# Exponentials of 1024 columns over a ring of two PSUM buffers, in attention with an interleaved projection

## What is computed

```python
xn = layernorm(x)
k, q, v = split(xn @ W_kqv.T, 3)                 # 16 heads of 64
bias = slope[h] * (n - s)                        # slope[h] = 2 ** (-(h + 1) / 2)
score = einsum('bhsd,bhnd->bhsn', q, k) / 32 + bias
s = einsum('bhsn,bhnd->bhsd', softmax(score), v) # keys n, queries s
g = silu(ffn(xn))                                # 3 cycles of a coupling network
out = x + s * g
```

## Time and profile before

| | us |
|---|---|
| median of the runs (2 runs, 2830.49 and 2832.97) | 2831.73 |
| profiled execution | 2836.87 |
| its span on the slowest core (core 1) | 2835.3 |
| spans of the 8 cores | 2811.7 to 2835.3 |

### The profile page before, as it was taken

One profiled execution on the slowest core, in us unless ns is written; L12 is line 12 of the kernel. 1 busy time (PEld: TensorE's weight loads), 2 busy tenths in 40 slices (PEclk: granted clock), 3 DMA queues, 4 the chain that ended last, 5 costly groups with the idle time before them and its releaser, 6 DMA issues.

```text
span 2835.3 us, 32583 instructions; the slowest of 8 cores (2811.7 to 2835.3 us)
## 1 busy us (share of the span) xinstructions
PE 2166.7 (76%) x8756; PEld 903.1 (32%) x8756; DVE 826.9 (29%) x1315; ACT 1466.6 (52%) x2366; POOL 100.7 (4%) x150
## 2 busy tenths in 40 slices
PE   0235889899899988998888855788888888854665
PEld 0232233233233223332222214433333333323444
DVE  1556323121111001010000006345345345345333
ACT  0220555768788898889999950133333333332000
POOL 1000000000000000000000000000000000002332
PEclk9667999999999899999999985799999999985555
DMA  9600211000000000000000024444444444433665
GB/s 186 164 30 8 49 28 23 16 11 14 8 8 8 8 8 8 1 9 8 8 9 9 8 56 163 123 108 104 102 110 101 104 110 99 107 72 128 195 194 177
DMA packets 343974, 190.21 MB, mean 67 GB/s; under 512 B 303419, under 2 KB 321981, under 8 KB 343694
## 3 DMA queue, kind: packets, MB, share of 16 engines
q1 hardware_dynamic: 323470, 160.08, 21.5%
q0 software_dynamic: 3696, 11.27, 2.8%
q10 hardware_dynamic: 16640, 16.78, 2.2%
HBM read 165.30 MB, written 36.96 MB: 71 GB/s over the span
## 4 chain that ended last, share of the span: by engine, by line
PE 46%; ACT 16%; DVE 15%; issue 11%; DMA 5%; DVEq 5%; POOL 1%; ACTq 1%; SPq 0%; another core or an unknown queue 0%; POOLq 0%
ACT PBUF L467 14%; PE PA L705 13%; PE PC L459 4%; PE PA L459 4%; PE PA L374 3%; PE PC L374 3%; PE PD L441 3%; DMA XT<-x 3%; PE PBp L441 3%; PE PD L443 2%; DVE STATE L821 2%; DVE TMP L812 2%; DVE SBF L790 2%; DVEq L824 2%; DVEq L818 2%
## 5 line engine op out<-in xcount | busy, mean ns | idle before, releaser
L467 ACT ACTIVATE PBUF<-PC,ebias_s 128x512 bf16<-128x512 f32 x977 | 665.0, 777 | 183.6 <-PE PC L459 115.1
L467 ACT ACTIVATE PBUF<-PA,ebias_s 128x512 bf16<-128x512 f32 x967 | 658.6, 774 | 139.3 <-PE PC L459 88.1
L459 PE MATMUL PC<-QT,KT 64*128 64x512 bf16 x977 | 344.7, 385 | 75.3 <-ACT PBUF L467 54.7
L705 PE MATMUL PA<-SBF,W1S 128*128 128x512 bf16 x1536 | 359.5, 398 | 25.6 <-DVE SBF L790 21.9
L459 PE MATMUL PA<-QT,KT 64*128 64x512 bf16 x967 | 317.3, 387 | 41.2 <-ACT PBUF L467 20.2
L716 ACT ACTIVATE H<-PA,b1c_s 128x512 bf16<-128x512 f32 x192 | 131.9, 687 | 348.1 <-PE PA L705 348.1
L812 DVE TENSOR_TENSOR TMP<-PD,STATE 128x512 f32<-128x512 f32 x192 | 123.7, 686 | 362.9 <-PE PD L804 357.5
L441 PE MATMUL PD<-PBUF,VB 128*65 128x512 bf16 x528 | 207.7, 393 | 27.1 <-ACT PBUF L467 17.0
L705 PEld LDWEIGHTS PA<-SBF,W1S 128*128 128x128 bf16 x1536 | 154.6, 102 | 230.7 <-issue 69.2
L487 DVE COPY SRW<-PBp 65x1024 f32<-65x1024 f32 x32 | 39.1, 1221 | 605.9 <-PE PD L443 605.9
L443 PE MATMUL PD<-PBUF,VB 128*65 128x512 bf16 x528 | 207.2, 392 | 0.0
(11 more groups left out here) (109 smaller groups left out, 1837.0 us busy)
## 6 DMA issues: line engine op xcount, KB each, us to landing
W1S<-w1b_s SPq DMA_DIRECT2D x192, 256.0 KB, 2.9
W2S<-w2b_s SPq DMA_DIRECT2D x96, 256.0 KB, 2.8
XTs<-x SPq DMA_DIRECT2D x8, 2048.0 KB, 28.1
sraw_s<-SRW SPq DMA_DIRECT2D x64, 256.0 KB
XT2s<-x SPq DMA_DIRECT2D x16, 1024.0 KB, 5.2
XT<-x SPq DMA_DIRECT2D x32, 512.0 KB, 4.1
SINB<-sraw_s ACTq DMA_DIRECT2D x16, 1024.0 KB, 6.2
out<-OUT SPq DMA_DIRECT2D x32, 512.0 KB, 2.9
```

The lines of the kernel that those rows point to most:

```text
L459: inst = TE.matmul(RING[r], lhs, QT[b][hh * 64:(hh + 1) * 64, sc * SC2:(sc + 1) * SC2], start=True, stop=True)
L467: inst = SE.activation(out=PB_[slot][:], in_=RING[r], func=AF.Exp, bias=ebias[:, h * 32 + nt: h * 32 + nt + 1], scale=1.0 / 32.0)
L705: inst = TE.matmul(HALF[slot][:], W1S[wslot][:, ft * 128:(ft + 1) * 128], sbf[:, ft * TC:(ft + 1) * TC], start=(ft == 0), stop=(ft == NF - 1))
```

## The change

Two neighbouring exponentials of a head become one. The ring is handed out to the attention in whole buffers, PA or PC (`ring_next_pair`): if the position is odd, it is rounded up to the next even one, a half being passed over; TensorE then waits for the tokens of both halves. Both score matmuls of a head are issued, only the second counts up tSC, and one ScalarE instruction reads 128x1024 out of PSUM and writes a buffer PBH of 1024 columns. Six PBH lie over the same bytes as the twelve PBUF. The two products read the two halves of PBH, and the tokens of both halves of the ring name that one exponential. The projection units still take single halves by `ring_next`. The order of the matmuls on TensorE is as before.

```diff
--- before.py
+++ after.py
@@ -132,6 +132,7 @@
     QT = [at(f"QT{i}", [128, S], BF16, 128 + 8 * i) for i in range(2)]
     VB = [at(f"VB{i}", [128, 32 * 130], BF16, 144 + 8.25 * i) for i in range(2)]
     PB_ = [at(f"PBUF{i}", [128, 512], BF16, 160.5 + 1 * i) for i in range(12)]
+    PBH = [at(f"PBH{i}", [128, 1024], BF16, 160.5 + 2 * i) for i in range(6)]
     SRW = [at(f"SRW{i}", [128, 1024], F32, 172.5 + 4 * i) for i in range(2)]
     VSTG = [at(f"VSTG{i}", [128, 512], F32, 180.5 + 2 * i) for i in range(2)]
     vsj = [0]
@@ -338,6 +339,19 @@
                 TE.wait_ge(sem.h, val)
             return r
 
+        PFULL = [PA, PC]
+
+        def ring_next_pair():
+            r = ring_pos[0]
+            if r % 2:
+                r = (r + 1) % 4
+            for q in (r, r + 1):
+                if ring_tok[q] is not None:
+                    sem, val = ring_tok[q]
+                    TE.wait_ge(sem.h, val)
+            ring_pos[0] = (r + 2) % 4
+            return r
+
         OUTH = [[PBp[0:65, 0:512], PBp[0:65, 512:1024]],
                 [PD[0:65, 0:512], PD[0:65, 512:1024]]]
         out_tok = [(vXBe, max(lnslot_tok[2], lnslot_tok[3])), None]
@@ -415,8 +429,8 @@
 
         SC2 = 512
         NSCP = 4
-        pb_av_tok = [0] * 12
-        pb_exp_tok = [0] * 12
+        pb_av_tok = [0] * 6
+        pb_exp_tok = [0] * 6
         srw_tok = [0, 0]
         sridx = [0]
 
@@ -431,21 +445,20 @@
                 def emit_attnv(flush=False):
                     while pend:
                         hh, pnt, pj = pend.pop(0)
-                        s0 = hh * 6 + (pj % 3) * 2
-                        TE.wait_ge(sExp.h, pb_exp_tok[s0 + 1])
+                        s0 = hh * 3 + (pj % 3)
+                        TE.wait_ge(sExp.h, pb_exp_tok[s0])
                         if not started[hh] and out_tok[hh]:
                             osem, oval = out_tok[hh]
                             TE.wait_ge(osem.h, oval)
                         st = not started[hh]
                         stop = flush and all(x[0] != hh for x in pend)
                         TE.matmul(OUTH[hh][0], v4[b][:, pnt, hh, 0:65],
-                                  PB_[s0][:], start=st, stop=stop)
+                                  PBH[s0][:, 0:512], start=st, stop=stop)
                         inst = TE.matmul(OUTH[hh][1], v4[b][:, pnt, hh, 0:65],
-                                         PB_[s0 + 1][:], start=st, stop=stop)
+                                         PBH[s0][:, 512:1024], start=st, stop=stop)
                         started[hh] = True
                         tAV.inc(inst)
                         pb_av_tok[s0] = tAV.n
-                        pb_av_tok[s0 + 1] = tAV.n
 
                 for nt in range(N0_PAIR[p], NT):
                     for hh in range(2):
@@ -453,23 +466,25 @@
                         if nt < N0[h]:
                             continue
                         lhs = KT[b][hh * 64:(hh + 1) * 64, nt * 128:(nt + 1) * 128]
+                        rp = ring_next_pair()
                         for sub in range(2):
                             sc = 2 * scp + sub
-                            r = ring_next()
-                            inst = TE.matmul(RING[r], lhs,
+                            inst = TE.matmul(RING[rp + sub], lhs,
                                              QT[b][hh * 64:(hh + 1) * 64, sc * SC2:(sc + 1) * SC2],
                                              start=True, stop=True)
-                            tSC.inc(inst)
-                            SE.wait_ge(tSC.h, tSC.n)
-                            slot = hh * 6 + (jj[hh] % 3) * 2 + sub
-                            if pb_av_tok[slot]:
-                                SE.wait_ge(tAV.h, pb_av_tok[slot])
-                            inst = SE.activation(out=PB_[slot][:], in_=RING[r], func=AF.Exp,
-                                                 bias=ebias[:, h * 32 + nt: h * 32 + nt + 1],
-                                                 scale=1.0 / 32.0)
-                            sExp.inc(inst)
-                            pb_exp_tok[slot] = sExp.n
-                            ring_tok[r] = (sExp, sExp.n)
+                        tSC.inc(inst)
+                        SE.wait_ge(tSC.h, tSC.n)
+                        slot = hh * 3 + (jj[hh] % 3)
+                        if pb_av_tok[slot]:
+                            SE.wait_ge(tAV.h, pb_av_tok[slot])
+                        inst = SE.activation(out=PBH[slot][:], in_=PFULL[rp // 2][:],
+                                             func=AF.Exp,
+                                             bias=ebias[:, h * 32 + nt: h * 32 + nt + 1],
+                                             scale=1.0 / 32.0)
+                        sExp.inc(inst)
+                        pb_exp_tok[slot] = sExp.n
+                        ring_tok[rp] = (sExp, sExp.n)
+                        ring_tok[rp + 1] = (sExp, sExp.n)
                     emit_attnv()
                     for hh in range(2):
                         if nt >= N0[2 * p + hh]:
```

## The result

The changed kernel takes 2891.35 us (median of 11 runs) against 2833.79 of the kernel before in the same series (10 runs); the ratio is 1.0205, with a 95% interval of 1.0189 to 1.0221. It is about 58 us slower, and the interval lies on both sides of 2%. The forecast was 2845, in a range of 2800 to 2885, and gave 0.82 to "within 2%". In some runs of either kernel the cores of one die have a lower clock and the run takes some per cent longer; the ratios leave such runs out, the medians do not.

The account below looks back on a forecast made before the run. ScalarE's exponentials bound steps without projection units, TensorE sets the pace with them; after the change a two-step buffer chain would. Terms −10.8 + 8.8 + 6.4 + 4.7 + 4 = +13 us on 2831.7 give 2845, range 2800 to 2885.

Parts of the forecast that it names:

- S0a to E0: In each step, from head 0's first score matmul to its exponential: 0.22 + 0.54 us.
- the alternation of short and long steps: Steps without projection units: S0 (head 0's score matmuls) starts at 0, 2.02, 4.53, 6.55 us and so on.
- the saving of 0.30 a step: Each two-head step: two wide exponentials for four narrow save 0.30 us, of which only 0.05 comes through.
- A: Rival, faster: in two-head steps the saving arrives whole, only engine rates count; 2742 us, chance 0.08.
- C: Rival, slower: an exponential's second PSUM bank costs a second access, +0.15 us on 444 steps; 2912 us, chance 0.04.
- Costed at nothing: Items priced at zero: single-head steps, two ring waits for one naming the same count, fewer ScalarE waits and increments.
- 4.53: Chain over two steps without units, through exponentials, score matmuls and attention-value products: 4.53 us, so 2.27 a step.
- −7.4 of pair 7: Pair 7's four strips without projection units: 73.5 us each against 75.34, −1.85 each.
- the +4 that was forecast: Pairs 0 to 3: 48 two-head steps at up to 0.2 us each and 16 short strips; bounds 0 and 10.
- rival B: Slower: TensorE's clock falls in a strip's first steps, pairs 4 to 7, 1.6 us lost a step; 2947 us, chance 0.06.
- its sign: What would show the clock falling: granted clock in pairs 6 and 7, now 0.99, below 0.95.
- the gains that I had subtracted: Pair 6: −1.2 us for strip ends and steps after the last unit, −1.85 for its strip without units.

Follow-up runs that it names:

- e2_coarse_narrow: e1_one_wait with two exponentials of 512 columns in place of each one of 1024, the ring still coarse; ratio 1.0399 to the kernel before.
- e5_wait_order: e1_one_wait, but where a buffer's halves carry different semaphores TensorE waits for the exponential's first and VectorE's copy last; 2853.15 us, ratio 1.0091.
- e9_before_two_waits: The kernel before, with every wait of TensorE on the ring issued twice with the same count; 2848.02 us, ratio 1.0057.
- e1_one_wait: The changed kernel, but where both halves of a buffer carry the same semaphore TensorE waits for it once, not twice; 2874.23 us, ratio 1.0143.
- e7_front_wide: e5_wait_order with all projection units of the next pair issued ahead of a pair's first step, none between steps; 2918.21 us, ratio 1.0320.

## Why the prediction was wrong

**What held.** Each term that had a row behind it came out: exponential 1.11 us (1.11 predicted), pitch 1.01 (1.006), S0a to E0 0.76 (0.22 + 0.54), the alternation of short and long steps, S1 waiting for VectorE's copy after a unit, and with one wait the distances 8.76, 6.25 and 16.30. The reading that the saving of 0.30 a step would not arrive was right, and e2_coarse_narrow shows why: the coarse ring costs more than the width gives. Rivals A and C are out: ScalarE saves its time and idles it away, and a read over two PSUM banks costs nothing beyond its columns.

**The step that failed** stands under "Costed at nothing": "two waits on the ring in place of one, which name the same count". I took a wait that is already satisfied for free. It stands behind the one that is not, in the very chain I had summed up, and adds about 0.1 us there: 4.53 becomes 4.62, which takes most of the forecast −7.4 of pair 7, and it comes once a step wherever units run: 8.76 becomes 9.00. By e5_wait_order it is worth 1.14%, 32 us of the 45 by which the forecast was short (some 5 of the 32 may be the clock, by the estimate below). That the same wait costs nothing in pair 7 of the kernel before (e9_before_two_waits) is the other half of the rule: there ScalarE sets the pace.

**Terms that were too small.** With one wait the ratio is 1.0091, 26 us, against my 13. By stage, e5_wait_order on its slowest core:

```profile
258.00:537.90 279.90, 247.15 (x974) 84.83 (x972) 80.88 (x107) 132.05 (x125) 0.00 (x0) 0.92 0.13 29
537.90:731.80 193.90, 175.20 (x690) 56.57 (x688) 31.90 (x49) 123.20 (x116) 0.00 (x0) 0.96 0.05 12
731.80:1045.50 313.70, 280.46 (x1106) 87.29 (x1104) 31.94 (x49) 231.90 (x221) 0.00 (x0) 0.98 0.03 8
1045.50:1396.90 351.40, 313.77 (x1248) 99.46 (x1248) 31.92 (x49) 267.28 (x256) 0.00 (x0) 0.99 0.03 7
1396.90:1695.80 298.90, 265.22 (x1018) 76.35 (x1018) 8.90 (x8) 264.73 (x256) 0.00 (x0) 0.98 0.03 8
```

That is +9.6, +7.3, +2.1, +12.5 and −2.1 against before, where +4, +4.7, +4.9, +7.0 and −7.4 were forecast. Single cores mislead here. The means over the eight cores, with the time at the lower clock in brackets (twice the stage's length times one less its granted clock):

| us | pairs 0 to 3 | pair 4 | pair 5 | pair 6 | pair 7 |
|---|---|---|---|---|---|
| before | 268.7 (27.8) | 186.0 (11.9) | 311.3 (26.0) | 340.1 (6.0) | 302.8 (11.9) |
| changed kernel | 283.1 (47.9) | 194.4 (7.3) | 326.4 (29.9) | 361.1 (13.2) | 301.1 (4.3) |
| e5_wait_order | 278.8 (43.4) | 191.4 (9.4) | 314.6 (14.9) | 350.9 (9.4) | 297.6 (12.4) |

*The clock, put at nothing in the sum.* In pairs 0 to 3 of the changed kernel the four cores with 53.2 us at the lower level take 285.5 us on the mean and the one with 37.5 takes 279.2. By these an estimate is 0.4 us of time for one at the lower level. The 16 us more of e5_wait_order then are some 6 of its +10.1, and what is left is the +4 that was forecast. This is rival B's loss, in another place and smaller than B had it: in pairs 6 and 7, where B named its sign, the granted clock of the changed kernel is 0.98 and 0.99. Why the lower level lasts longer in pairs 0 to 3 no run shows. Nor is the clock at the strips' starts of pair 7 new. There e5_wait_order takes 73.4 to 73.7 us a strip where the clock holds and 74.8 to 75.9 where it does not, as three us of such a strip of e1_one_wait show (75.2 us, core 0):

```profile
1415.00:1418.00 3.00, 2.90 (x8) 0.80 (x10) 0.00 (x0) 2.08 (x2) 0.00 (x0) 0.54 0.70 154
```

But five of the eight cores of the kernel before have such strips too, 76.1 to 76.9 us in place of 75.3. Its slowest core, from whose rows I took the 75.34, is not one of them; here are 50 us on core 0, one that is, with a strip's start at 1517 us and a granted clock of 0.93:

```profile
1500.00:1550.00 50.00, 44.82 (x165) 13.62 (x164) 2.35 (x2) 47.45 (x83) 0.00 (x0) 0.93 0.05 11
```

On the mean pair 7 gained 5.2 us. Over the whole attention the lower level takes 84 us before and 90 in e5_wait_order, so by the same estimate the clock is only 2 of the 26 us; it moved between the stages.

*The ends of the strips.* Pair 6 on core 3 is 350.1 us in place of 339.0. From the first q/k unit to the first v tile there are +5.5 (4.8 forecast), from the first v tile to the eighth +5.2 (4.6), and in all the rest, the beginning, the last tile, and the steps and strip ends behind it, +0.4, where −2.4 was forecast. The strip without units took 74.7 us, not 73.5. So in pair 6 the units were priced about right, and most of the miss is in the gains that I had subtracted. For the other stages this was not traced, and stays open.

**The chances.** The range (2800 to 2885, the likeliest case 2825 to 2865) was drawn round a sum without the second wait, since what stands under "Costed at nothing" had no upper bound at all. Had the wait been bounded by the nearest row, the 0.14 us from an exponential's end to the matmul, on each of 444 steps, the range would have reached past 2890. The 0.82 for "within 2%" was too sure for the same reason; the measured ratio lies at 2%, on neither side of it for certain.

## What to carry to other kernels

Before making an instruction wider, find the chain through the buffers that it frees. If the wider one frees them later, that chain may become the bound, and only the difference between the old bound and this chain arrives, here 0.05 of 0.30 us a step. Count every wait that is issued behind one that lets go late, even where it asks for what has already come, and issue the late one last. Compare a stage over all cores, with its granted clock, before reading a few us of difference as an effect of the change. And where two changes pull apart in different stages, as here with and without projection units, choose by stage.

## What the runs showed of the hardware

A wait of TensorE on a semaphore costs about 0.1 us behind another, with the same semaphore and the same count: 0.250 us from the exponential's end to the matmul with two, 0.144 to 0.145 with one (medians over pair 7, in the changed kernel and e9_before_two_waits, and in the kernel before, e1_one_wait and e5_wait_order). The page counts no busy time for it, so it shows only as a longer gap.

An exponential that reads 128x1024 out of PSUM takes 1.11 us and follows the one before by 1.01, where two of 128x512 take 1.157.

TensorE's granted clock can stay at its lower level through whole strips in which it hardly pauses: with S0, AV0, S1, AV1 it stayed at 0.50 for 120 us and more, the matmul rows covering 70.00 of 70 us, while the order S0, S1, AV, AV left that level in its first two-head steps in the strips looked at here (e7_front_wide at 918 to 921 us, after 20 us). What came before was in both the strip's start, where TensorE waits for VectorE's copies and the first exponentials. Begun later, at full speed, the new order kept it. Why the one order rises and the other does not is not shown by these runs.
